# A sixth thread for the last batch's mixture and attention, and norm statistics taken on ScalarE

## The reference

```python
x = x + 0.5 * ffn(layernorm(x))          # "front": weights and activations in blockwise fp4, inner width 704
x = x + mamba(layernorm(x))              # projection, conv, dt ("head"), then a selective scan over 512 steps ("scan")
x = x + 0.5 * ffn(layernorm(x))          # "back": the same FFN, the same weights
x = x + 0.5 * lora_mixture(layernorm(x)) # 8 experts of rank 8, softmax router
x = x + attention(layernorm(x))          # 16 heads of width 16, alibi, causal
x = x + 0.5 * lora_mixture(layernorm(x))

def _layernorm(x, axis=-1, eps=1e-05):
    m = jnp.mean(x, axis=axis, keepdims=True)
    v = jnp.var(x, axis=axis, keepdims=True)
    return (x - m) / jnp.sqrt(v + eps)
```

## Time and profile before

| | before |
|---|---|
| runs | 4396.26, 4398.87, 4400.55 us: median 4398.87 |
| profiled execution, its own time | 4389.99 us |
| its span | 4388.2 us |
| TensorE busy | 3951.7 us (90%) |
| VectorE busy | 3874.2 us (88%) |
| ScalarE busy | 2369.7 us (54%) |
| GpSimd busy | 1722.5 us (39%) |

### The profile page before, as it was taken

The page is one execution under the profiler, slowest core; times in us unless marked ns, Lnnn a source line. Parts: engine busy times, 40 slices in busy tenths (PEclk is TensorE's granted clock), DMA queues, the critical chain, the costliest instruction groups (busy, mean ns, idle before and its releaser), DMA issues.

```text
span 4388.2 us, 56065 instructions
## 1 busy us (share of the span) xinstructions
PE 3951.7 (90%) x19171; PEld 2042.4 (47%) x19171; DVE 3874.2 (88%) x5708; ACT 2369.7 (54%) x4341; POOL 1722.5 (39%) x1293
## 2 busy tenths in 40 slices
PE   5878889999999899999999999999989999999998
PEld 3333444444545454454545445454544545454554
DVE  7699999899999989999898999999898999988622
ACT  2444455656555565646546565655656565565433
POOL 1254434443444434343443434443443444343200
PEclk9989999999999999999999999999999999999999
DMA  2698787878778787877897787797886878878301
GB/s 63 160 206 212 171 209 171 204 158 191 178 173 204 170 202 176 201 185 159 205 182 187 166 198 174 160 228 144 207 182 162 196 172 209 171 205 181 84 21 44
DMA packets 241442, 753.53 MB, mean 172 GB/s; under 512 B 37650, under 2 KB 132659, under 8 KB 171524
## 3 DMA queue, kind: packets, MB, share of 16 engines
q1 hardware_dynamic: 241156, 749.95, 73.3%
HBM read 647.30 MB, written 101.71 MB: 171 GB/s over the span
## 4 chain that ended last, share of the span: by engine, by line
DVE 35%; PE 33%; DMA 12%; ACT 8%; issue 8%; SPq 3%; POOL 2%; DVEq 0%; ACTq 0%; POOLq 0%
DVE state L1733 10%; DVE mt L1812 6%; DMA state<-dtx_scratch 5%; PE m L1217 4%; DVE u L1728 3%; DMA decay<-dt_scratch 3%; PE m L1244 3%; PE pd L1443 2%; PE y L1318 2%; PE y L1306 2%; DMA gz_scratch<-front 2%; DVE front L1667 2%; PE m L1259 1%; SPq L713 1%; DVE front L1638 1%
## 5 line engine op out<-in xcount | busy, mean ns | idle before, releaser
L797 POOL TENSOR_TENSOR state<-state,bc 128x1024 f32<-128x1024 f32 x512 | 1266.3, 2474 | 1308.1 <-DVE u L1728 1299.0
L1733 DVE TENSOR_TENSOR_SCAN state<-decay,u 128x1024 f32<-128x1024 f32 x512 | 1165.7, 2277 | 4.6 <-issue 0.2
L1018 ACT ACTIVATE decay<-decay,a_neg 128x511 f32<-128x511 f32 x1024 | 675.5, 713 | 188.5 <-DMA decay<-dt_scratch 188.1
L1217 PE MATMUL m<-w_gu,hats_m 128*128 128x480 f32 x1472 | 682.3, 584 | 64.4 <-DVE front L1642 45.0
L1728 DVE TENSOR_TENSOR u<-state,bc 128x1024 f32<-128x1024 f32 x512 | 640.1, 1250 | 51.0 <-DMA state<-dtx_scratch 45.2
L1217 PEld LDWEIGHTS m<-w_gu,hats_m 128*128 128x128 f32 x1472 | 257.0, 192 | 335.5 <-issue 159.8
L1164 PE MATMUL y<-minus,zero 128*128 128x512 bf16 x1556 | 406.7, 388 | 2.1 <-ACT vec L872 2.1
L778 POOL TENSOR_TENSOR front<-front,hsc_m 128x704 f32<-128x704 f32 x128 | 200.6, 1567 | 517.3 <-DVE front L1547 517.3
L1244 PE MATMUL m<-w_dn,front 128*128 128x256 f32 x1476 | 366.7, 390 | 16.0 <-ACT front L951 14.6
L1306 PE MATMUL y<-state,sel 128*32 128x512 f32 x2048 | 280.6, 621 | 50.3 <-POOL state L797 50.0
L1244 PEld LDWEIGHTS m<-w_dn,front 128*128 128x128 f32 x1476 | 270.1, 192 | 100.4 <-ACT front L951 48.5
(11 more groups left out here) (320 smaller groups left out, 7177.3 us busy)
## 6 DMA issues: line engine op xcount, KB each, us to landing
decay<-dt_scratch SPq DMA_DIRECT2D x256, 1024.0 KB, 7.4
state<-dtx_scratch SPq DMA_DIRECT2D x256, 1024.0 KB, 11.6
qk_scratch<-shared SPq DMA_DIRECT2D x64, 384.0 KB, 3.8
shared<-qk_scratch SPq DMA_DIRECT2D x384, 64.0 KB
kh<-qk_scratch SPq DMA_DIRECT2D x384, 64.0 KB
xs_scratch<-front SPq DMA_DIRECT2D x16, 1024.0 KB, 9.3
dt_scratch<-front SPq DMA_DIRECT2D x256, 64.0 KB, 4.8
dtx_scratch<-hats_m SPq DMA_DIRECT2D x256, 64.0 KB, 6.5
```

The costliest lines, as they stand in the source:

```text
L797: eng.tensor_tensor(st, st, bc[:, 1:2, :].to_broadcast([P, WIDE, L]), ALU.mult).then_inc(scan_pool.sem, scan_pool.step(f"c{r}{h}"))
L1018: ins = eng.activation(d, d, ACT.Exp, scale=a_neg[:, g:g + 1])
L1217: mm = eng.matmul(f.bank(r, f"gu{t}{p}")[:, 0:2 * width], norm.hat_t[:, k, t * P:(t + 1) * P], w_gu[:, k, 2 * lo:2 * (lo + width)], start= ...
L1733: eng.tensor_tensor_scan(st, decay[:, n % ND, h * WIDE * L:(h + 1) * WIDE * L], u[:, :], 0.0, ALU.mult, ALU.add).then_inc(scan_dve.sem, sc ...
```

## The change

**Norms.** The norms of heads and back FFNs (32 of the 96) leave VectorE. The residual copies that end a front FFN (line 955) or a scan (line 1024) now write their row sums through `accum_out`; the scan's become four copies of 128x256 in place of two of 128x512. ScalarE then takes minus the mean (`less`, 128x4) and four Square activations of x - mean (128x256, written where the hats will go) with `accum_out` for the sum of squares. GpSimd forms the variance from these and continues as before, without its own `less`. `buffer_free`, the wait for the buffer that hats are written to, stands ahead of the squares. The front norms stay as they were.

**Sixth thread.** Batch 15's mixture, attention and second mixture are taken from thread 2 and become a thread of their own, with its own semaphores and scratch in DRAM, and with buffers in memory that is dead once the last scan is over: `qh` and `pt` in `state`, `kh` and the hats in `decay`, `va` and `gm` in `w_in`, the ends in `skip`, the small tiles in `gate`; its banks are the two of `u` and `Y` in place of `PG`, `PU`, `PD`, and its attention turns over four banks (`u`, `u`, `m0`, `m1`). All `ORDER` strings are written anew. TensorE has 166 `keeper` matmuls fewer (1552 in place of 1718).

```diff
-                self.pool = Steps(sem(f"norm_pool_{tag}"), ["less", "var", "rstd", "bias"])
+                self.pool = Steps(sem(f"norm_pool_{tag}"), ["less"] * (tag[0] != "m") + ["var", "rstd", "bias"])
+                if tag[0] == "m":
+                    self.squares = sb(f"squares_{tag}", [P, T])
+                    self.less_done, self.square = sem(f"norm_less_{tag}"), sem(f"norm_square_{tag}")
...
+        sums = {w: sb(f"sums_{w}", [P, T]) for w in ("back", "head")}
...
+        squared_before = lambda w, n: sum(v != "front" and WORK.index((v, m)) % 2 == WORK.index((w, n)) % 2 for v, m in WORK[:WORK.index((w, n))])
...
         skip = sb("skip", [P, C, L])
         gate = sb("gate", [P, 2, L])
...
-        qk_scratch = nc.dram_tensor("qk_scratch", [4, 3, P, L], BF16, kind="Internal").ap()
+        last_small = [gate[:, 1, :], 0]
...
+        nr_late = Norm("late", flat(decay)[:, 2048:4096], late)
...
+        va_late = flat(w_in)[:, 0:T * H * (HD + 1)].rearrange("p (t h c) -> p t h c", t=T, h=H)
+        gm_late = flat(w_in)[:, 1088:1088 + T * (E * R + 1)].rearrange("p (t c) -> p t c", t=T)
+        last = big_parts(flat(state), flat(decay)[:, 0:2048].bitcast(BF16).rearrange("p (b g l) -> p b g l", b=2, g=G), flat(skip)[:, 0:2 * L],
+                         va_late, gm_late, gate[0:3 * G, 0, 0:L // 2].bitcast(BF16))
+
...
+        A = Att(key="pd", nr=nr, PG=PG[:, :], PU=PU[:, :], PD=PD[:, :], banks=[PG[:, :], PU[:, :]], **main, **small_parts(sb), **own("main"), **steps("main"))
+        Z = Att(key="y", nr=nr_late, PG=U[0], PU=U[1], PD=Y[:, :], banks=U + [m[:, :] for m in MB], **last, **small_parts(late), **own("last"), **steps("last"))
...
-        att_banks = lambda r: [PG, PU] + (MB + [u[:, 0:L], u[:, L:2 * L]] if r == B - 1 else [])
-
-        def att_bank(r, event):
-            banks = att_banks(r)
-            return banks[att_events.index(event) % len(banks)]
...
             def third():
-                for i in range(B):
-                    yield from lora(i, 2 * i, 3 * i)
-                    yield from attention(i, 3 * i + 1)
-                    yield from lora(i, 2 * i + 1, 3 * i + 2)
-
-            weave(order, first(), second(), third(), ahead(), fifth(), *idle)
+                for i in range(B - 1):
+                    yield from lora(A, i, 2 * i, 3 * i)
+                    yield from attention(A, i, i, 3 * i + 1)
+                    yield from lora(A, i, 2 * i + 1, 3 * i + 2)
+
+            def sixth():
+                yield from lora(Z, B - 1, 0, 0)
+                yield from attention(Z, B - 1, 0, 1)
+                yield from lora(Z, B - 1, 1, 2)
+
+            weave(order, first(), second(), third(), ahead(), fifth(), sixth(), *idle)
...
+            def rstd_of_squares(n, q, squared):
+                yield
+                eng.wait_ge(n.square, squared)
+                eng.tensor_scalar(n.var[:, :], n.squares[:, :], 1.0 / D, EPS, ALU.mult, ALU.add).then_inc(n.pool.sem, n.pool.step("var"))
+                yield
+                yield from root(n, q)
...
             def lead(w, n, norm, q):
-                yield from rstd(norm, q)
+                if w == "front":
+                    yield from rstd(norm, q, fronts_before(n), False)
+                else:
+                    yield from rstd_of_squares(norm, q, squared_before(w, n) + 1)
...
+            def hats(n, q, x, buffer_free=None, total=None, uses=0):
+                if total is not None:
+                    yield
+                    eng.wait_ge(*total[1])
+                    eng.activation(n.less[:, :], total[0][:, :], ACT.Copy, scale=-1.0 / D).then_inc(n.less_done, 1)
+                    for t in range(T):
+                        yield
+                        if t == 0:
+                            if buffer_free:
+                                buffer_free()
+                            eng.wait_ge(n.less_done, uses + 1)
+                        ins = eng.activation(n.hat[:, t, :], x[:, t, :], ACT.Square, bias=n.less[:, t:t + 1], accum_out=n.squares[:, t:t + 1])
+                        if t == T - 1:
+                            ins.then_inc(n.square, 1)
                 for t in range(T):
                     yield
...
-                        if buffer_free:
+                        if buffer_free and total is None:
                             buffer_free()
                         eng.wait_ge(n.pool.sem, n.pool.after(q, "bias"))
                     eng.activation(n.hat[:, t, :], x[:, t, :], ACT.Identity, bias=n.bias[:, t:t + 1], scale=n.rstd[:, t:t + 1]
...
-                yield from hats(norm, q, xx[:, n % NX, :, :], dtx_stored)
+                total = {"front": None, "back": (sums["back"], (scan_act.sem, scan_act.after(n, "res3"))),
+                         "head": (sums["head"], (f.low_act.sem, f.low_act.after(FFNS.index(("front", n)), f"res{T - 1}")))}[w]
+                yield from hats(norm, q, xx[:, n % NX, :, :], dtx_stored, total, total and squared_before(w, n))
...
-                    eng.activation(x[:, t, :], f.bank(r, f"dn{t}")[:, 0:D], ACT.Copy).then_inc(f.low_act.sem, f.low_act.step(f"res{t}"))
+                    if FFNS[r][0] == "front":
+                        if t == 0 and n:
+                            eng.wait_ge(normed("head", n - 1)[0].less_done, squared_before("head", n - 1) + 1)
+                        eng.activation(x[:, t, :], f.bank(r, f"dn{t}")[:, 0:D], ACT.Copy, accum_out=sums["head"][:, t:t + 1]
+                                       ).then_inc(f.low_act.sem, f.low_act.step(f"res{t}"))
+                    else:
+                        eng.activation(x[:, t, :], f.bank(r, f"dn{t}")[:, 0:D], ACT.Copy).then_inc(f.low_act.sem, f.low_act.step(f"res{t}"))
...
+                for t in range(T):
+                    yield
+                    if t == 0 and i:
+                        eng.wait_ge(normed("back", i - 1)[0].less_done, squared_before("back", i - 1) + 1)
+                    eng.wait_ge(scan_pe.sem, scan_pe.after(i, f"o{t // 2 * 2 + 1}"))
+                    eng.activation(xx[:, i % NX, t, :], Y[:, t % 2 * D:(t % 2 + 1) * D], ACT.Copy, accum_out=sums["back"][:, t:t + 1]
+                                   ).then_inc(scan_act.sem, scan_act.step(f"res{t}"))
+
...
-                yield
-                if w == "front" and n:
-                    eng.wait_ge(x_loaded, 16 * n)
-                if w == "back":
-                    eng.wait_ge(scan_act.sem, scan_act.after(n, "res1"))
-                if w == "head":
-                    eng.wait_ge(f.low_act.sem, f.low_act.after(FFNS.index(("front", n)), f"res{T - 1}"))
-                yield from norm(norm_of, q, xx[:, n % NX, :, :])
+                if w == "front":
+                    yield
+                    if n:
+                        eng.wait_ge(x_loaded, 16 * n)
+                    yield from norm(norm_of, fronts_before(n), xx[:, n % NX, :, :])
```

The rest of the diff passes the set (`A` or `Z`, here `s`) through `lora` and `attention` on every engine, and replaces the strings, of which these are two lines of VectorE's end:

```diff
-        "22222221111122121222222222222111111222222211112222122223333333322333332332300000000000220022022022020022002000202202202202202000"
...
+        "22022022000000000000055555555222555255552222222222255552555522222222225555225555252555555555555555552252522222555555555555522255"
```

760 lines of the change are left out of this document (390 added, 370 removed).

## The result

The changed kernel takes 4382.4 us (median of 20 runs, 4351.9 to 4401.6) beside 4403.5 us of the kernel before (median of 20, 4384.0 to 4417.8). The ratio is 0.9949 (95% interval 0.9932 to 0.9966): 22 us, 0.5% faster. 4307 was forecast, a gain of 92; the measured one is a quarter of that and lies outside the range of 4275 to 4345.

A forecast was written before the change was run, and what follows sets the result against it. VectorE was taken to bound the overlapped part, a chain of dependent steps the end. Gains of 51 us (norms) and 41 (tail), 92 in all, took 4390.0 to 4298, as a median 4307; range 4275 to 4345.

The forecast's parts named there:

- So in this stretch VectorE is the bound: Overlapped part, 168 to 4092 us: VectorE, busy 93.3%, sets the limit; TensorE's real work is only 82%.
- the 51 us: Overlapped part: gain from taking 30 norms off VectorE, 1.74 us each plus waits; between 26 and 78.
- The VectorE time is given back: Rival, overlapped part: freed VectorE time turns into waits such as for dtx; 20 of 51 us stay, 4338; chance 0.16.
- TensorE's clock falls: Rival, tail: with fewer zero matmuls the mean clock falls to 0.88, costing 26 us, 4333; chance 0.07.
- The tail, 41 us: From batch 15's last scan residual to the end: 240 us, 41 less than the 281.2 before.
- The FFN's window: Tail, batch 15's last scan residual to its last FFN residual: expected 73 us, with part of batch 14's attention moved out.
- the chain behind it: Tail, batch 15's last FFN residual to the end: 149.6 us alone plus 17 for colliding work, 167.
- Two attentions collide: Rival, tail: batch 14's and 15's attentions get in each other's way; tail saves only 10 us, 4338; chance 0.12.
- One bound of this sum: Tail: upper limit of the gain, put at 65 us with nothing colliding at all.
- The low end of the range: Whole kernel: 4275 us, from fuller gains of 60 us in the overlapped part and 64 in the tail.
- ScalarE, 90 us (75 to 127): ScalarE's added work for squares, `less`, smaller residual copies and row sums, expected to be hidden in its idle time.
- Slower: Rival: squares on in-order ScalarE delay decays and copies, VectorE waits 4 us more per norm, 4426; chance 0.04.

The follow-up runs named there:

- e1: Kernel before, own order, statistics of the head and back norms left out of VectorE with nothing in their place: 4402.2 us, ratio 0.9990.
- e9: Kernel before with every fourth zero matmul ahead of the last scan's end left out (378 fewer): 4427.9 us, ratio 1.0044.
- e4: Changed kernel with every fourth zero matmul issued twice throughout (1940 in place of 1552): 4353.9 us, ratio to the kernel before 0.9897.
- e7: Changed kernel with every fourth zero matmul issued twice only ahead of batch 15's last scan residual: 4356.6 us, ratio to the kernel before 0.9903.
- e6: Kernel before with every fourth zero matmul issued twice (2147 in place of 1718): 4394.3 us, ratio 0.9975.
- e3: Changed kernel with less, squares and row sums left out of ScalarE, nothing in their place: 4376.2 us, ratio to the kernel before 0.9944.
- e11: Changed kernel without ScalarE's less, squares and row sums, every fourth zero matmul doubled ahead of batch 15's last scan residual: 4360.0 us, ratio to the kernel before 0.9888.
- e2: Kernel before, own order, no sixth thread, with head and back norms taken on ScalarE as in the changed kernel: 4444.2 us, ratio 1.0097.

## Why the prediction was wrong, point by point

**The step that failed is the first: "So in this stretch VectorE is the bound", and with it the 51 us.** The removed work was sized rightly: 52 us less busy on the page. Leaving it out alone (e1) gave 0.1%, at most 11 us of the 51, and its waits grew by as much. In a usual execution the overlapped part did not get 51 us shorter but some 26 longer. A share of 93.3% said that VectorE was full, not that it set the pace. Each engine has its instructions in a fixed order and waits at hundreds of places for another; before, TensorE was busy 3577 of 3924 us with its zero matmuls, and its 160 us at the lower clock were part of that. The reading that I chose took the zero matmuls out of TensorE's load and called the rest room. That room is not all free: e9 shows that 378 fewer of them cost 19.5 us.

**"The VectorE time is given back"** (0.16) is what happened, though not by 31 us but nearly wholly, and the waits are not for dtx, which are unchanged beside the one ahead of the first scan, but for ScalarE's and, less, for TensorE's results. The 45.2 us that I read as waits of the overlapped part hold the 14.7 of that one.

**"TensorE's clock falls" (0.07)** was the right mechanism at the wrong place. It was priced in the tail, from the 181 zero matmuls that are gone there. The tail's clock did fall, 1.00 and then 0.94, and the tail was still at its forecast; e4, with more zero matmuls there, and e7, without, differ by no more than the noise. It was the overlapped part, with 1% more of them than before, whose time at the lower level grew: 256 us for 160 in the profiled pair, and by the medians of the clock, 0.974 and 0.968, less than half as much more. That this costs time is shown: a quarter more zero matmuls brought 20 us by the ratios (e7), a quarter fewer in the kernel before cost 19.5 (e9). That the new order puts other gaps on TensorE which they do not cover fits this but is argued. Whether the clock is all of it stays open: with a quarter more in both kernels the new order's overlapped part is still 8 to 14 us longer, no more than the noise of the two (e7, e6). The Trainium skill, TensorE: Matmul & The Clock Gate, section What's actually happening, has the clock follow how busy the engine has recently been: the trace agrees in kind, with a lower clock where zero matmuls were left out (e9, 0.9645 for 0.974) and a higher one where they were added (e6, 0.980 for 0.975; e7, 0.9765 for 0.968). Their count alone, from which I judged, is not enough: the changed kernel has more of them there and the lower clock.

**The tail, 41 us**: right, 47. The FFN's window 68.1 for 73, the chain behind it 166.0 for 167. Taking a third of the moved work as colliding was near enough; attention 15 took 4359.5 - 4246.1 = 113.4 us with company and four banks, 104.4 alone with six. "Two attentions collide" did not come. One bound of this sum is wrong by its own terms: with nothing colliding, 281.2 - 59 - 149.6 is a gain of 73 and not 65. The low end of the range, which takes 64 from it, would lie lower; the measured time lies on the other side.

**ScalarE, 90 us (75 to 127)**: 78 on the page. A square took 502 ns and its accumulator read 194 ns, of which part lies beside the next square, so that the page's sum is smaller than that of the instructions:

```profile
L939 ACT ACTIVATE hats_m<-xx,less_m 128x256 f32<-128x256 f32 x128 | 63.4, 502 | 1.7 <-DMA dtx_scratch<-hats_m 0.6
...
L939 ACT ACTIVATION_READ_ACCUMULATOR hats_m<-xx,less_m 128x1 f32 x128 | 24.8, 194 | 0.0
```

The high end had been right to give each `accum_out` 0.2 us. The estimate from the Trainium skill, ScalarE: Activation LUTs, section What ACT_TABLE_LOAD costs, had 492 ns for the square; the trace has 502. That this is hidden was right in the new order (e3, e11) and wrong in the old one (e2): **"Slower"**, squares ahead of decays, is the likely reading of e2, 43 us over before with 45.0 us of waits for decays, of which e1 has 22.7 without squares.

What is left open is why the new order has the lower clock, that is which moves of its strings made it. With a quarter more zero matmuls (e7) the overlapped part is as long as that of the kernel before without them, not shorter, and whether an order exists in which the 52 us of VectorE are worth something was not tried.
